# Two of four folding products moved into the first tile, the up tables ahead of it, the weight identities on VectorE

## The reference, cut to what matters

```python
x = x + attention(x)                  # q,k,v = x@Wq.T, x@Wk.T, x@Wv.T; rms norm and rotation of q, k; 64 new
                                      # rows go into a block cache; window of 256; softmax; @Wo.T
x = x + x @ weights[s]                # s = one of 8 subjects of each window; a 64x64 product over channels
x = x + x @ W_base.T + ((x @ Wt.T) @ A[e2].T @ B_w[e2].T @ Wp.T) * s2[e2]     # e2 of 4, rank 16
x = x + x @ W.T + (x @ A3[e3].T) @ B3[e3].T * s3[e3]                          # e3 of 8, rank 16
```

## Time and profile before

| | |
|---|---|
| median of 3 runs | 456.7 us (456.54 to 456.89) |
| the profiled execution, its own time | 458.0 us |
| its span | 456.2 us |
| TensorE busy | 440.8 us, 97% of the span |
| VectorE, ScalarE, GpSimd busy | 68%, 57%, 50% |
| chain that ended last | TensorE 90%, VectorE 3%, GpSimd 2% |

### The profile page before, as it was taken

How to read it: one execution, slowest core, us unless ns; L and a number is a source line. 1 busy time by engine, 2 the same in 40 slices (tenths; PEclk the granted TensorE clock), 3 DMA queues, 4 the chain that set the end, 5 groups by cost and what they waited for, 6 DMA issues and landing times.

```text
span 456.2 us, 10436 instructions
## 1 busy us (share of the span) xinstructions
PE 440.8 (97%) x3039; PEld 316.7 (69%) x3039; DVE 308.8 (68%) x899; ACT 262.0 (57%) x772; POOL 228.5 (50%) x245
## 2 busy tenths in 40 slices
PE   8999996999699999999999999999999999999996
PEld 3444884466377778777877777777777787777764
DVE  4688878655667677776767676767777676757531
ACT  0756850354357575756666475757575666656641
POOL 0225469665655657374655655564747465341000
PEclk9999997999899999999999999999999999999998
DMA  6577796264826465565647373746456563533131
GB/s 211 192 246 250 214 349 200 85 175 109 272 62 185 93 170 130 143 163 112 178 91 209 62 214 65 198 102 166 134 137 145 138 197 72 158 61 66 28 70 53
DMA packets 75593, 67.40 MB, mean 148 GB/s; under 512 B 50869, under 2 KB 51253, under 8 KB 75538
## 3 DMA queue, kind: packets, MB, share of 16 engines
q1 hardware_dynamic: 60208, 37.97, 30.9%
q0 software_dynamic: 14400, 28.05, 22.6%
q10 hardware_dynamic: 930, 0.72, 0.6%
HBM read 72.49 MB, written 10.22 MB: 181 GB/s over the span
## 4 chain that ended last, share of the span: by engine, by line
PE 90%; DVE 3%; issue 2%; POOL 2%; DMA 1%; ACT 1%; DVEq 0%; POOLq 0%; ACTq 0%
PE gb L1152 13%; PE sbk L1322 10%; PE ob L1346 10%; PE tb L1335 9%; PE gb L1181 7%; PE gb L1390 7%; PE gb L1157 6%; PE tb L1308 5%; PE gb L1395 4%; PE gb L1369 3%; PE gb L1400 3%; PE ob L1145 2%; PE ob L1380 2%; PE gb L1204 2%; PE sbk L1209 1%
## 5 line engine op out<-in xcount | busy, mean ns | idle before, releaser
L1031 DVE CUSTOM_DVE_ANT_0 wide<-sbk,mask 128x336 f32<-128x336 f32 x128 | 60.0, 505 | 63.4 <-PE sbk L1322 63.1
L728 ACT ACTIVATE pt_s<-tb 112x384 f32<-112x384 f32 x128 | 55.6, 488 | 53.5 <-PE tb L1335 53.5
L722 ACT ACTIVATE wide<-wide,negmax 128x336 f32<-128x336 f32 x128 | 72.6, 571 | 22.0 <-DVE negmax L1031 21.2
L526 POOL DMA_INDIRECT windows_more<-newkv,idx_b x48 | 49.0, 1021 | 61.9 <-issue 50.1
L526 POOL DMA_INDIRECT windows<-newkv,idx_b x48 | 49.8, 1038 | 47.7 <-issue 40.4
L1335 PEld LDWEIGHTS tb<-cst_late,wide 128*112 128x112 f32 x384 | 44.4, 133 | 18.9 <-issue 11.1
L1335 PE MATMUL tb<-cst_late,wide 128*112 128x128 f32 x384 | 52.5, 273 | 2.3 <-DVE wide L1044 1.5
L1322 PE MATMUL sbk<-kt_s,qt_s 64*128 64x336 f32 x256 | 52.8, 489 | 0.0
L1044 DVE TENSOR_SCALAR wide<-wide,rinv 128x336 f32<-128x336 f32 x128 | 45.4, 397 | 2.3
L716 ACT ACTIVATE kt_s<-tb 128x336 f32<-128x336 f32 x64 | 25.4, 449 | 13.3 <-PE tb L1308 13.2
L1181 PE MATMUL gb<-wkv_s,xt_s 128*128 128x512 f32 x72 | 31.9, 596 | 0.0
(11 more groups left out here) (217 smaller groups left out, 1026.8 us busy)
## 6 DMA issues: line engine op xcount, KB each, us to landing
xt_s<-xt_dram SPq DMA_DIRECT2D x31, 256.0 KB, 4.7
newkv<-kvo SPq DMA_DIRECT2D x16, 256.0 KB, 3.6
xtok_s<-xtok_dram SPq DMA_DIRECT2D x16, 256.0 KB
up_sel<-up_tab SPq DMA_DIRECT2D x128, 32.0 KB
out_dram<-xo SPq DMA_DIRECT2D x16, 256.0 KB, 4.1
down_sel<-down_tab SPq DMA_DIRECT2D x64, 32.0 KB
wkv_s<-wkv_dram SPq DMA_DIRECT2D x4, 256.0 KB, 6.1
wide<-wt_dram SPq DMA_DIRECT2D x4, 256.0 KB, 5.3
```

Of the source, the lines that this page charges most:

```text
L526: nc.gpsimd.indirect_dma_start(kv_s[r][:, c, :], None, newkv, bass.IndirectOffsetOnAxis(ap=idx_b[r][:, (1, 2, 4)[c]:(1, 2, 4)[c] + 1], axi ...
L722: nc.scalar.activation(prob[i][:, g, :], neg_s[:, g, :], ACT.Exp, bias=negmax[:, g:g + 1], scale=-1.0, accum_out=psum_p[i][:, g:g + 1]).th ...
L728: nc.scalar.activation(pt_s[g][:], tb[g % 2][0:KP, 0:CH * 128].rearrange("p (c q) -> p c q", c=CH), ACT.Copy).then_inc(S["pt_ev"], 1)
L1031: V.tensor_tensor_reduce(out=neg_s[:, g, :], in0=sbk[g % 2][:, 0:WK], in1=mask[(t.part(u) + k) % 2][:], scale=-1.0 / 16, scalar=3.0e38, op ...
```

## The change

- The identities are added by VectorE, behind key tiles 13 and 14, and the loads of `late_pieces` begin two tiles earlier (`LATE_A` = 8).
- Of the four folding products two stay in the head, back to back; `fold(2)` and `fold(3)` stand in the first tile, where `layer1` and `layer3` stand in the others. Their parts m_hi and m_lo are made there as well.
- The product of the queries of tile 0 follows the first two folds; their transposes stand behind `down3` and `cross`.
- The four `carried` products, `up2` and `cross` come before the first tile, in four different banks; `carry(0)` to `carry(3)` follow the first two norms.
- On GpSimd the gathers of window 1 come behind `lay_over` of window 0, and the scaling of `b3_s` behind the first q_rstd.
- The tile buffers are laid out so that x1, x2, up_sel, xtok and others lie over `wb_s` and `w3_s`, which are now read until the fourth fold; SP therefore waits for the four folds (`m23_mm`) before the first xtok load, and ScalarE for the stored tables (`tabs_stored`) before the first ot_hi.

```diff
-        LATE_A = TILES // 2 + 2
+        LATE_A = TILES // 2
...
+                if first:
+                    sp.wait_ge(S["m23_mm"], C)
                 after(sp, S["x1_ready"], t.n(1, 0))
                 sp.dma_start(xtok_s[:], xtok[t.n(1, 0)]).then_inc(S["l_xtok"], 16)
...
             root("k", 4, 16)
-            add_identity(wb_s, ("l_wb", 16 * C), "wb_ident")
-            add_identity(w3_s, ("l_w3", 16 * C), "w3_ident")
-            gather_pair(t0, 0, 1)
-            gather_single(t0, 0, 1)
...
             lay_over(t0, 0, 0)
+            gather_pair(t0, 0, 1)
+            gather_single(t0, 0, 1)
             root("q", 8, 1)
+            pool.wait_ge(S["l_scl"], 48)
+            pool.wait_ge(S["l_ab3"], 32)
+            P.tensor_scalar(b3_s[:], b3_s[:], scl3[:], 1.0, ALU.mult, ALU.mult).then_inc(S["b3_scaled"], 1)
             lay_over(t0, 0, 1)
...
             for n in range(SPLIT_A - 1, TILES):
                 if n + 3 < TILES:
                     xk_low(n + 3)
                 key_tile(n)
+                if n == 13:
+                    add_identity(wb_s, "l_wb", "wb_ident")
+                elif n == 14:
+                    add_identity(w3_s, "l_w3", "w3_ident")
...
                 def between():
                     if first:
-                        carry(0)
-                        carry(1)
+                        m23_low(2, gb[1])
...
                 if first:
-                    carry(2)
-                    carry(3)
+                    m23_low(3, ob[1])
...
                 probs_t(t, 1, 0)
                 probs_t(t, 1, 1)
+                if first:
+                    m23_high(3, ob[1])
                 if not last:
                     queries(t.n(1, 2), t.b(1, 4, 4), gb[1])
...
                 probs_t(t, 0, 2, False)
                 probs_t(t, 0, 3, False)
-                if not first:
+                if first:
+                    pe.wait_ge(S["up_ev"], NE3 // 2)
+                    fold(2, gb[1])
+                else:
                     layer1(t)
                 scores(t, 0, 1, (0, 1))
                 values(t, 0, 0)
                 values(t, 0, 1)
-                if first:
-                    carried(0)
-                    carried(1)
-                else:
+                if not first:
                     ranks(t)
                 scores(t, 0, 1, (2, 3))
                 if not last:
                     keys_t(t, 1, 1)
-                if not first:
+                if first:
+                    fold(3, ob[1])
+                else:
                     layer3(t, not last)
                 probs_t(t, 1, 0, last)
                 probs_t(t, 1, 1, last)
```

More of the change, by code:

```diff
@@ L287, in build @@
         mask = [sb(f"mask{i}", [128, WK]) for i in range(2)]
-        xtok_s = sb("xtok_s", [128, 512])
         down_sel = [sb(f"down_sel{i}", [128, C, 64]) for i in range(2)]
-        pt_s = [sb(f"pt_s{i}", [KP, CH, 128]) for i in range(G)]
-        up_sel = [sb(f"up_sel{i}", [128, 512]) for i in range(2)]
-        ot_s = [sb(f"ot_{w}", [128, 4, 128], f32r) for w in ("hi", "lo")]
         x1 = sb("x1", [128, 512])
@@ L297, in build @@
         xo = sb("xo", [128, 512])
+        up_sel = [sb(f"up_sel{i}", [128, 512]) for i in range(2)]
+        xtok_s = sb("xtok_s", [128, 512])
+        sb("rest_of_w3", [128, 64])
+        ot_s = [sb(f"ot_{w}", [128, 4, 128], f32r) for w in ("hi", "lo")]
+        sb("tables_below", [128, (NE2 + NE3) * C * RANK + C * 128 + 512 + 64 + NE3 * 64 + C * 64])
+        pt_s = [sb(f"pt_s{i}", [KP, CH, 128]) for i in range(G)]
         gb = [ctx.enter_context(nc.psum_tensor(f"gb{i}", [128, 512], f32)) for i in range(2)]
@@ L494, in _ @@
                             con("ident", NB)[:, 0:NB].unsqueeze(1).to_broadcast([NB, BLOCKS, NB]), ALU.mult).then_inc(S["blkd_ready"], 1)
-            def add_identity(w, loaded, done):
-                pool.wait_ge(S[loaded[0]], loaded[1])
-                for c in range(C):
-                    d = w[:, c, 128 * c:128 * c + 128]
-                    last = P.tensor_tensor(d, d, ident, ALU.add)
-                last.then_inc(S[done], 1)
             def copy_index(t, u, k):
@@ L988, in _, with add_identity @@
             key_tile(8)
+            def add_identity(w, loaded, done):
+                dve.wait_ge(S[loaded], 16 * C)
+                for c in range(C):
+                    d = w[:, c, 128 * c:128 * c + 128]
+                    last = V.tensor_tensor(d, d, ident, ALU.add)
+                last.then_inc(S[done], 1)
             for n in range(SPLIT_A - 1, TILES):
@@ L1066, in tile @@
                 if first:
-                    dve.wait_ge(S["cross_ev"], 1)
-                    V.tensor_tensor(cross_s[:], cross[:].unsqueeze(1).to_broadcast([128, NE3, 64]),
-                                    con("hot3").unsqueeze(2).to_broadcast([128, NE3, 64]), ALU.mult).then_inc(S["cross_ready"], 1)
+                    for e in range(NE3 // 2):
+                        carry(e)
                 inverse(t, 0, 0, 1)
@@ L1433, in tile @@
                     else:
[L1434 removed]
+                        pe.wait_ge(S["m23_lo"], 3)
                     queries_t(t.n(1, 2), gb[1])
[L1436 to L1439 removed]
+                if not first:
                     layer3_low(t)
@@ L1466, in _ @@
                   lambda c: w3_s[:, c, :]).then_inc(S["up2_mm"], 1)
-            pe.wait_ge(S["m23_lo"], C)
-            dense(ob[1][:, 0:64], lambda c: a3_s[:, c, :], lambda c: up2t_s[:, c, 0, :]).then_inc(S["cross_mm"], 1)
+            for g in (0, 2):
+                scores(t0, 0, 0, (g, g + 1))
+            for e in range(NE3 // 2):
+                carried(e)
             pe.wait_ge(S["split_lo"], len(splits))
```

87 lines of the change are left out of this document (31 added, 56 removed).

## The result

The changed kernel takes 451.98 us, median of 4 runs (451.66 to 452.70), against 456.62 (456.53 to 456.89) for the kernel before beside it: 4.64 us less, a ratio of 0.9887 (95% interval 0.986 to 0.9914). It is faster, but by little more than half of the 8.6 us predicted; the time lies above the range. The profiled execution has a span of 450.0 us and a time of its own of 451.83.

A forecast was written before the change was run, and what follows sets the result against it. TensorE was taken as the bound, with gains between the key tiles and tile 1: 11.77 us of idle and low clock removed, 3.15 of waits added, net 8.6, so 456.7 becomes 448.1 us; range 446.4 to 451.2.

The forecast's parts named there:

- Removed waits: TensorE between the key tiles and tile 1: 8.28 us of idle and 3.49 of low clock go.
- hidden, barely: Second query transpose: 12.1 us of TensorE work covers VectorE's 11.1 us chain, so the 1.99 us wait goes.
- GpSimd's next powers ... lose nothing.: Last key tiles: GpSimd's powers start at 66.28 and 68.91, after VectorE's identity adds end at 66.1 and 68.8; no loss.
- 4 us or more to spare: Loads of the folding weights, issued two key tiles earlier, land by 61.5, in time for the identities.
- Rival E: Identities not early because loads are late or hold up key tiles: up to 3.50 + 1.91 stays, 449 to 453.5; chance 0.05.
- New waits: TensorE before tile 1: 1.05 us before the third head's score, 2.1 for norms behind the fourth fold; together 3.15.
- Work: TensorE's full-clock work between the key tiles and tile 1 stays at 46.16 us.
- Window 0's rows ... I take 0.: First key transposes: gathered rows come at 80.3, TensorE wants them at 80.5; wait 0, range 0 to 2.5 us.
- rival C: Window 0's rows are late: with a store of 5.9 us TensorE waits 2.5, giving 450.6 us; chance 0.13.
- nothing competes with these gathers any more: Argument against late rows for window 0: GpSimd's gathers there run unhindered; no size of its own.
- Rival B: The clock falls at the new 2.1 us wait among transposes, costing 1.6 us: 449.7 us; chance 0.20.

The follow-up runs named there:

- e4: The kernel before, with only the identities added by VectorE instead of GpSimd, between the last key tiles: 458.10 us against 463.14, ratio 0.9887.
- k1: The changed kernel itself, run again unaltered as a base on a third chip: 452.63 us beside 456.94 for the kernel before.
- k2: The changed kernel with VectorE's four q angle tables moved ahead of the last key tiles, on the third chip: 449.48 us against 452.63 for the changed kernel.
- e3: The changed kernel with the loads of wb and w3 put back two key tiles later, as before the change: 459.65 us on a chip with engine stand-stills.
- e2: The changed kernel with VectorE's four q angle tables moved ahead of the last key tiles, first of three such runs: first gather 1.06 us instead of 3.34.
- c2: The changed kernel with the q angle tables written in place by an operation with one SBUF input: first gather 1.33 us against 3.34, wait 0.47.

## Why the prediction failed, point by point

- **Removed waits.** Right for this profile: 3.50, 1.03, 1.99, 1.51 and the clock of the first fold are gone, and e4 shows 4.9 us of it to be the identities'. For the 1.99 it is luck. The walk that called it "hidden, barely" had VectorE's steps alone in it; GpSimd's q_rstd comes last, and as soon as TensorE comes earlier it waits again, 0.51 in k1 and 1.62 in k2. These, done at 70.0 instead of 68.8, still precede the fold.
- **"GpSimd's next powers ... lose nothing."** Wrong by a little: 1.48 and 1.53 where the earlier trace rows had 1.26, beside VectorE's work.
- **The loads, "4 us or more to spare".** Right for their own landing, wrong as a free edit: they hold up the stores of the key rows, and ScalarE's kvo buffer with them. 0.81 in the trace, gone in e3. Rival E had named it at 0.05.
- **New waits.** Right: 0.84 for a gap of 0.9, 2.10 for 2.1. Where TensorE comes earlier the 2.10 shrinks (1.30 in k1, 0.47 in k2), as the wait above grows.
- **Work.** 124.66 - 71.47 less 6.20 of idle and 1.63 of clock is 45.4, where the sum had 46.16: 0.8 in the kernel's favour.
- **"Window 0's rows ... I take 0."** This is the step that failed: a wait put at 0 measured 3.01. By medians the chain ended 0.2 us before TensorE asked. Of its terms the start was 1.1 late (75.19 for 74.1), the distance from first to third gather 5.37 for 3.1, and the third gather's way to TensorE 3.73 for 3.1: 4.0 in all, less the 0.2 and the 0.8 by which TensorE asked later. The distance is the term that matters: e2 has it at 3.1 again, starts as late (75.68), and waits 0.20. The sentence that set rival C at 0.13, "nothing competes with these gathers any more", was the error: the changed order brought the gathers onto the four q angle tables, and e2 and c2 show that these hold them. Rival C's own way to be late, a slow store, didn't come about: from store to gather it took 75.19 - 72.20 = 3.0. I had the rule before me, and dismissed it on one row where VectorE kept its 0.28 beside a gather: that row says what VectorE loses, not what the gather does.
- **The clock.** Rival B priced a fall at the new 2.10; it did not come there in this profile, but behind the 3.01, which rival C had priced without it.

The account: 0.77 (key tiles) + 3.01 + 1.63 - 0.21 (first new wait smaller) - 0.8 (work) = 4.4, and tile 1 is late by 124.66 - 120.3 = 4.36. The time missed 451.98 - 448.1 = 3.9, so by the medians 0.4 to 0.5 came back behind tile 1. By the two profiles it is more: tile 1 begins 4.2 earlier than before and the span ends 6.2 earlier, 456.2 to 450.0. There the profile of before has granted clocks of 0.73 and 0.70 at 446 to 452 us, and this one has 1.00 in its last stretch of work; single executions can't settle that.

## What to carry to other kernels

When a wait goes, walk the next chain with the durations that it will have beside its new neighbours, not with medians from where it stood; above all where GpSimd's gathers come forward onto VectorE operations with two SBUF inputs. A cover of 0.2 us is no cover: give such a chain a chance near one half, and price it with the clock that may fall behind it. And ask of an edit that is off the path, such as an earlier load, what shares its queue.

## What the runs showed of the hardware that I had not expected

- A gather's instruction on GpSimd took 1.06 us with VectorE's four two-input operations moved away and 3.2 to 3.3 beside them, repeated on three chips; beside the same four, but started 0.18 behind the first instead of 0.09, it took 1.37 (e4).
- The same wait of 3.0 us has the clock at its lower level behind it in six profiles and at its full level in one.
- On two chips TensorE, ScalarE and VectorE stood still together in the first tile, while GpSimd went on: VectorE's longest gap there is 3.7 to 8.8 us in the changed kernel and its repairs, and 3.5 where nothing stands still. The kernel before takes 463 to 464 us there, against 457 on the third. The cause stays open; it was not tried.
